# Quantised attention with its loop written out, two heads scored side by side, and its weights turned as pairs of bytes

## The reference, cut to what matters

```python
q = (x @ Wq + bq).reshape(1, B * N, H, hd)
kv = (cond @ Wkv + bkv).reshape(1, -1, 2, H, hd)
...
q = _fq_sym(q, axis=-1)        # rounded to -127..127 times a scale
k = _fq_sym(k, axis=-1)
v = _fq_sym(v, axis=2)
attn = jnp.einsum('bhqd,bhkd->bhqk', q, k)
attn = jax.nn.softmax(attn.astype(jnp.float32), axis=-1)
attn = _fq_unsigned(attn, axis=-1)   # each row: round(w / (max/255)), 0..255
out = jnp.einsum('bhqk,bhkd->bqhd', attn, v)
return out @ Wp + bp
```

## Time and profile before

| | us |
|---|---|
| median of 3 runs | 3037.68 (3037.57 to 3043.3) |
| profiled execution | 3038.51 |
| its span, first to last instruction | 3036.7 |
| VectorE busy over the span | 1932.5 (64%) |
| TensorE busy over the span | 2498.7 (82%) |
| ScalarE busy over the span | 1482.0 (49%) |
| GpSimd busy over the span | 409.3 (13%) |

### The profile page before, as it was taken

How to read it: one execution, slowest core, us unless ns; L and a number is a source line. 1 busy time by engine, 2 the same in 40 slices (tenths; PEclk the granted TensorE clock), 3 DMA queues, 4 the chain that set the end, 5 groups by cost and what they waited for, 6 DMA issues and landing times. The chain is left out here.

```text
span 3036.7 us, 50228 instructions
## 1 busy us (share of the span) xinstructions
PE 2498.7 (82%) x16570; PEld 1358.9 (45%) x16570; DVE 1932.5 (64%) x3686; ACT 1482.0 (49%) x2055; POOL 409.3 (13%) x454
## 2 busy tenths in 40 slices
PE   6874775999979999999664888787878865999998
PEld 3333554555547777777552222222222232444444
DVE  6995556667743333333456998888888845666665
ACT  5552332444433333333232776666666633666664
POOL 0001220111012222333133000000000001001100
PEclk9886776999979999999776555555555567999999
DMA  2000000000010000000000999999999940000001
GB/s 83 0 0 19 0 0 12 16 26 21 21 29 18 18 17 17 17 17 9 21 0 18 177 176 169 165 169 162 171 163 171 173 71 17 24 23 16 23 23 36
DMA packets 594876, 175.35 MB, mean 58 GB/s; under 512 B 548642, under 2 KB 594212, under 8 KB 594724
## 3 DMA queue, kind: packets, MB, share of 16 engines
q1 hardware_dynamic: 594724, 173.44, 29.6%
HBM read 37.07 MB, written 2.10 MB: 13 GB/s over the span
## 5 line engine op out<-in xcount | busy, mean ns | idle before, releaser
L1682 DVE TENSOR_SCALAR_CACHE_REDUCE ctxT<-psum,e_nsq 128x1024 f32<-128x1024 f32 x512 | 637.2, 1282 | 74.2 <-issue 54.1
L1651 PE MATMUL psum<-e_KT,e_Qs 48*128 48x512 bf16 x1024 | 519.9, 611 | 181.7 <-DVE ctxT L1682 151.0
L1703 ACT ACTIVATE xh<-ctxT,e_ebias 128x2048 uint16<-128x2048 f32 x128 | 256.2, 2002 | 134.0 <-DVE e_ebias L1686 134.0
L1703 ACT ACTIVATE xl<-ctxT,e_ebias 128x2048 uint16<-128x2048 f32 x128 | 256.2, 2002 | 119.2 <-DVE e_ebias L1686 119.2
L1651 PEld LDWEIGHTS psum<-e_KT,e_Qs 48*128 48x128 bf16 x1024 | 67.3, 104 | 415.8 <-issue 408.1
L103 PE MATMUL psum<-xh,d_WT 128*128 128x512 f16 x768 | 229.4, 381 | 2.6 <-DVE d_WT L1214 2.6
L1662 PEld LDWEIGHTS psum<-e_Vi,xnT 128*128 128x128 f16 x4096 | 129.5, 105 | 216.8 <-issue 216.8
L1233 DVE TENSOR_TENSOR d_ACC<-psum,d_ACC 128x512 f32<-128x512 f32 x128 | 82.5, 686 | 171.1 <-PE psum L1287 171.1
L103 PE MATMUL psum<-xh,f_WA 128*128 128x512 f16 x544 | 152.7, 383 | 13.9 <-DVEq L1896 11.8
L103 PE MATMUL psum<-xh,c_Wx 128*128 128x512 f16 x576 | 161.3, 383 | 0.8 <-DVE X L960 0.8
L1662 PE MATMUL psum<-e_Vi,xnT 128*128 128x16 f16 x4096 | 152.5, 175 | 8.1 <-DMA xnT<-xh 4.5
(11 more groups left out here) (312 smaller groups left out, 4965.9 us busy)
## 6 DMA issues: line engine op xcount, KB each, us to landing
d_Wn<-in_L_attn_w_qkv SPq DMA_DIRECT2D x16, 384.0 KB, 3.2
f_W<-in_L_ffn_w_routed SPq DMA_DIRECT2D x32, 176.0 KB, 2.5
ctx_rows<-in_ctx SPq DMA_DIRECT2D x1, 2048.0 KB, 8.6
X<-in_x SPq DMA_DIRECT2D x1, 2048.0 KB, 14.0
c_Wgu<-in_L_ffn_rg SPq DMA_DIRECT2D x16, 128.0 KB, 2.1
c_Wgu<-in_L_ffn_rw SPq DMA_DIRECT2D x16, 128.0 KB, 2.2
c_Wd<-in_L_ffn_rw SPq DMA_DIRECT2D x16, 128.0 KB, 2.2
d_Wn<-in_L_attn_w_gate SPq DMA_DIRECT2D x16, 128.0 KB, 3.0
```

The costliest lines, as they stand in the source:

```text
L1651: mm = pe.matmul(m.bank[b + q], Qs[rows, x.u // 2 % QSLOTS, :], KTt[rows, j // 2, (2 * hf + q) * BLK:(2 * hf + q + 1) * BLK], start=True, ...
L1682: dve.tensor_scalar(S32[:, sl, hf * HALF:(hf + 1) * HALF].rearrange("p (a b) -> p a b", a=2), m.psum[:, b:b + 2, :], nsq[:, ds(x.n(), 1)], ...
L1703: act.activation(e16[x.u % SLOTS], S32[:, x.u % 2, :], ACT.Exp, bias=ebias[:, x.u % 2:x.u % 2 + 1], scale=-1.0, accum_out=esum[:, ds(x.n() ...
```

## The change

- The loop is written out: 256 units on every engine, no hardware loop and no `wait_apart`; semaphores are waited for at constants. TensorE reads the queries straight from `e_QT`, and GpSimd's copies into `e_Qs` go.
- Two heads are scored at once: `score` is called once for two units and alternates the matmuls of the even head (rows 0 to 47) and the odd head (rows 64 to 111), each into banks of its own. The ring still has three pairs of banks, now counted in chunks (even half 0, odd half 0, even half 1, odd half 1). VectorE takes four chunks out per two units.
- The bias of the exponential moves from VectorE to GpSimd (L1598 of the changed kernel).
- ScalarE writes the integers as bytes; the DMA turns them as pairs, 8 blocks of 128 x 128 two-byte numbers a unit; GpSimd then casts 2048 bytes a row to bfloat16, in order (L1591), three units late (`LATE`). So that a pair of bytes belongs to two tiles of keys, ScalarE stores `e_KT` with the tokens of two tiles interleaved. TensorE reads the weights of a tile with a step of two numbers. `e_Vi` is bfloat16.
- Four slots instead of two for the scores (a new tensor `e_Smore`) and the biases; `LAG` is 7; the 2^24 is gone.

```diff
@@ -1385,7 +1385,7 @@
 
         QT = sb("QT", [P, NT * PR, P], BF16)
         KTt = sb("KT", [P, PR, TOK], BF16)
-        Vi = sb("Vi", [P, KT, H, HD], F16)
+        Vi = sb("Vi", [P, KT, H, HD], BF16)
         sq = sb("sq", [P, NT * H])
         nsq = sb("nsq", [P, NT * H])
         sv = sb("sv", [P, D])
@@ -1463,8 +1463,10 @@
                             b = 4 + 2 * (tt % 2)
                             act.activation(QT[:, ds(t * PR, PR), :].rearrange("p a b -> p (a b)"),
                                            m.bank[b].bitcast(BF16), ACT.Copy)
-                            act.activation(KTt[:, :, ds(t * P, P)], m.bank[b + 1].bitcast(BF16)
-                                           .rearrange("p (a b) -> p a b", a=PR), ACT.Copy).then_inc(stored, 1)
+                            act.activation(KTt[:, :, ds(i * 2 * TPB * P + tt // 2 * 2 * P, 2 * P)]
+                                           .rearrange("p a (q b) -> p a q b", b=2)[:, :, :, tt % 2],
+                                           m.bank[b + 1].bitcast(BF16).rearrange("p (a b) -> p a b", a=PR),
+                                           ACT.Copy).then_inc(stored, 1)
 
                 @block.vector
                 def _(dve):
@@ -1554,49 +1556,24 @@
 
 
         N = NT * H
-        BODY, SLOTS, LAG, QAHEAD, QSLOTS = 48, 4, 6, 3, 6
-        Qs = sb("Qs", [P, QSLOTS, P], BF16)
-        mn = sb("mn", [P, 2, 2])
-        ebias = sb("ebias", [P, 2])
+        SLOTS, LAG, LATE = 4, 7, 3
+        mn = sb("mn", [P, SLOTS, 2])
+        ebias = sb("ebias", [P, SLOTS])
         esum = sb("esum", [P, N])
         Osb = sb("Osb", [P, NT, D])
-
-
-        S32 = m.ctxT
-        PT = m.xnT[:, :, :].rearrange("p a b -> p (a b)").bitcast(F16).rearrange("p (s k q) -> p s k q", s=SLOTS, k=KT)
-        e16 = [x[:, :, :].rearrange("p a b -> p (a b)").bitcast(U16)[:, i * TOK:(i + 1) * TOK]
-               for x in (m.xh, m.xl) for i in range(2)]
-
-
...
-        def loop(eng, step, extra=0):
-
...
+        Smore = sb("Smore", [P, 2, TOK])
+
+
+        S32 = [m.ctxT[:, 0, :], m.ctxT[:, 1, :], Smore[:, 0, :], Smore[:, 1, :]]
+        PT = m.xnT[:, :, :].rearrange("p a b -> p (a b)").bitcast(BF16).rearrange("p (s k) -> p s k", s=SLOTS)
+        e8 = m.xh[:, :, :].rearrange("p a b -> p (a b)").bitcast(U8).rearrange("p (s k) -> p s k", s=SLOTS)
+        P8 = m.xl[:, :, :].rearrange("p a b -> p (a b)").bitcast(U16).rearrange("p (s c q) -> p s c q", s=SLOTS, c=KT // 2)
+
+
+        def loop(step, extra=0):
+
+            for n in range(N + extra):
+                step(n)
 
         def pair_banks(c):
 
@@ -1606,106 +1583,103 @@
             @block.gpsimd
             def _(pool):
 
...
+                def unpack(n):
+                    sl = n % SLOTS
+                    pool.wait_ge(laid[sl], 16 * (n // SLOTS + 1))
+                    if n >= SLOTS:
+                        pool.wait_ge(mixed, n - SLOTS + 1)
+                    pool.tensor_copy(PT[:, sl, :],
+                                     P8[:, sl, :, :].rearrange("p c q -> p (c q)").bitcast(U8)).then_inc(unpacked, 1)
+
+                def step(n):
+                    if n < N:
+                        sl = n % SLOTS
+                        pool.wait_ge(score_out, n // 2 * 4 + 3 + n % 2)
+                        pool.tensor_scalar(ebias[:, sl:sl + 1], mn[:, sl, 0:1], mn[:, sl, 1:2], LN255,
+                                           ALU.min, ALU.add).then_inc(biased, 1)
+                    if n >= LATE:
+                        unpack(n - LATE)
+                loop(step, LATE)
 
             @block.sync
             def _(sp):
-                def step(x):
-                    m.wait_apart(sp, exped, x.n() + 1)
-                    if x.at_least(SLOTS):
-                        m.wait_apart(sp, mixed, x.n() - (SLOTS - 1))
-                    sp.dma_start_transpose(PT[:, x.u % SLOTS, :, :], e16[x.u % SLOTS].bitcast(F16)).then_inc(laid[x.u % SLOTS], 16)
-                loop(sp, step)
+                def step(n):
+                    sl = n % SLOTS
+                    sp.wait_ge(exped, n + 1)
+                    if n >= SLOTS:
+                        sp.wait_ge(unpacked, n - SLOTS + 1)
+                    sp.dma_start_transpose(P8[:, sl, :, :], e8[:, sl, :].bitcast(U16)).then_inc(laid[sl], 16)
+                loop(step)
 
             @block.tensor
             def _(pe):
-                def score(x):
-                    j = x.j
-                    rows = slice(64 * (j % 2), 64 * (j % 2) + 48)
-                    if j % 2 == 0:
-                        m.wait_apart(pe, q_here, x.n(2) + 1)
+                def score(n):
+
                     for hf in range(2):
-                        if x.at_least(2):
-                            m.wait_apart(pe, score_out, x.n(1, 2) + hf - 2)
-                        elif 2 * x.u + hf >= 3:
-                            pe.wait_ge(score_out, 2 * x.u + hf - 2)
-                        b = pair_banks(2 * x.u + hf)
+                        c = 2 * n + 2 * hf
+                        if c >= 2:
+                            pe.wait_ge(score_out, c - 1)
                         for q in range(2):
-                            mm = pe.matmul(m.bank[b + q], Qs[rows, x.u // 2 % QSLOTS, :],
-                                           KTt[rows, j // 2, (2 * hf + q) * BLK:(2 * hf + q + 1) * BLK],
-                                           start=True, stop=True)
+                            col = (2 * hf + q) * BLK
+                            for odd in range(2):
+                                rows = slice(64 * odd, 64 * odd + 48)
+                                mm = pe.matmul(m.bank[pair_banks(c + odd) + q], QT[rows, n // 2, :],
+                                               KTt[rows, n % H // 2, col:col + BLK], start=True, stop=True)
                         mm.then_inc(scored, 1)
 
-                def mix(x):
-                    j = x.j
-                    m.wait_apart(pe, laid[x.u % SLOTS], x.n(SLOTS, 16) + 16)
-                    if j % 8 == 0 and x.at_least(16):
-                        m.wait_apart(pe, normed, x.n(8) - 1)
+                def mix(n):
+                    j = n % H
+                    pe.wait_ge(unpacked, n + 1)
+                    if j % 8 == 0 and n >= 16:
+                        pe.wait_ge(normed, n // 8 - 1)
                     for k in range(KT):
-                        mm = pe.matmul(m.bank[6 + j // 8][:, j % 8 * HD:(j % 8 + 1) * HD], PT[:, x.u % SLOTS, k, :],
+                        mm = pe.matmul(m.bank[6 + j // 8][:, j % 8 * HD:(j % 8 + 1) * HD], PT[:, n % SLOTS, k // 2 * 2 * P + k % 2:(k // 2 + 1) * 2 * P:2],
                                        Vi[:, k, j, :], start=(k == 0), stop=(k == KT - 1))
                     mm.then_inc(mixed, 1)
 
-                def step(x):
-                    if x.exists():
-                        score(x)
-                    if x.back(LAG).exists():
-                        mix(x.back(LAG))
-                loop(pe, step, LAG)
+                def step(n):
+                    if n % 2 == 0 and n < N:
+                        score(n)
+                    if n >= LAG:
+                        mix(n - LAG)
+                loop(step, LAG)
 
             @block.vector
             def _(dve):
-                def step(x):
-                    sl = x.u % 2
-                    if x.at_least(2):
-                        m.wait_apart(dve, exped, x.n() - 1)
+                def step(n):
+                    if n % 2:
+                        return
+                    if n >= SLOTS:
+                        dve.wait_ge(exped, n - SLOTS + 2)
                     for hf in range(2):
-                        b = pair_banks(2 * x.u + hf)
-                        m.wait_apart(dve, scored, x.n(1, 2) + hf + 1)
-                        dve.tensor_scalar(S32[:, sl, hf * HALF:(hf + 1) * HALF].rearrange("p (a b) -> p a b", a=2),
-                                          m.psum[:, b:b + 2, :], nsq[:, ds(x.n(), 1)], None, ALU.mult, ALU.min,
-                                          accum_out=mn[:, sl, hf:hf + 1]).then_inc(score_out, 1)
-                    m.wait_apart(dve, score_out, x.n(1, 2) + 2)
-                    dve.tensor_scalar(ebias[:, sl:sl + 1], mn[:, sl, 0:1], mn[:, sl, 1:2], LN255,
-                                      ALU.min, ALU.add).then_inc(biased, 1)
-                loop(dve, step)
+                        dve.wait_ge(scored, n + hf + 1)
+                        for odd in range(2):
+                            sl = (n + odd) % SLOTS
+                            b = pair_banks(2 * n + 2 * hf + odd)
+                            dve.tensor_scalar(S32[sl][:, hf * HALF:(hf + 1) * HALF].rearrange("p (a b) -> p a b", a=2),
+                                              m.psum[:, b:b + 2, :], nsq[:, n + odd:n + odd + 1], None, ALU.mult, ALU.min,
+                                              accum_out=mn[:, sl, hf:hf + 1]).then_inc(score_out, 1)
+                loop(step)
 
             @block.scalar
```

(86 more changed lines are left out.)

1 line of the change is left out of this document (removed).

## The result

The changed kernel takes 2875.77 us (median of 4; 2874.03 to 2879.97) against 3038.53 before: ratio 0.9463, 95% interval 0.9447 to 0.948. The forecast was 2910 in a range of 2850 to 3060, faster. The direction held, and so did the reading that VectorE's chain sets the pace; the gain was 163 us where 127 were worked out, and the stall at each turn-around with TensorE, on which the forecast rested, was nearly absent.

A forecast was written before the change was run, and what follows sets the result against it. VectorE's own chain was taken as the bound: 128 pairs x 5.22 = 668 against 795.9 gives -128, with -0.3 at the start and +1 at the tail -127, so 2910 us; range 2850 to 3060.

The forecast's parts named there:

- What bounds the kernel: VectorE's chain of two take-outs and a bias sets 3.10 us a unit; DMA near second, share 1.01 at 2.9.
- Two heads at once: Scoring: a group of four matmuls lasts 1.01 like two; a pair of units takes 5.22, a unit 2.61.
- the 1.40: TensorE-VectorE turn-around: 0.23 to the group's start plus 1.17 to VectorE's, against 1.21 for one take-out.
- Bias to GpSimd, loop written out: VectorE loses 256 biases of 213 ns, the wait before them and 0.23 gaps; two take-outs, 2.42 a unit, remain.
- The cast: GpSimd's cast of 2048 numbers takes 1.9 us; two units need 4.6 of 5.22, so it is covered.
- The mixes and the weights' step: TensorE's two mixes take 1.1 at 32 ns a load despite the stepped read; slack 0.6, so no cost.
- The rival's upper price: Stepped weight loads on TensorE at 107 ns each: 6.9 a pair of units, 3128 us; chance 4%.
- half-speed rival: Stepped weight loads on TensorE at 64 ns: next group 0.3 late, 5.5 a pair, 2950 us; chance 7%.
- The DMA: Transposes move 8 blocks instead of 16; landing between 4.3 and half of it, covered by about 5 us or more.
- The tail: End of block: last cast 1.9 and late bias 1.2 against about -2 of transpose: +1 on 9.3.
- The clock: TensorE's granted clock stays 0.50, as it will be busy about 3.2 of 5.22, less than today's 78%.
- a risen clock: Rival: TensorE's clock at 1.00, group about 0.6, no stall, VectorE at 2.42 a unit: 2861 us; chance 9%.

The follow-up runs named there:

- the step of eight: Changed kernel with TensorE's weights read eight numbers (16 bytes) apart instead of two, output differs: 2948.66 us.

## Why the prediction was right, and where its size was off

- *What bounds the kernel:* right. VectorE's chain set the pace before and does after. The DMA was the near second, but its capacity was misread: with sixteen bits it gave a unit in 2.64, not 2.93.
- *Two heads at once,* the term that was mis-sized: 2 x (1.40 + 1.21) = 5.22 a pair, measured 4.95. 128 x 0.27 is 35 us, and the forecast was 34 high. The stall of 0.19 at every turn-around did not come: 0.01 is left in the middle of a pair, and the 0.10 at its head is a second wait on one instruction. Both parts of the 1.40 were read from rows whose waits had a semaphore instruction beside them, which the change removes; with it back, 1.44 and 5.30 were measured. The diff named that instruction and I priced it only as part of "the loop's bookkeeping". The overlap of the row halves held (1.03 for four matmuls). But the pairing, for which that overlap was needed, bought nothing: one head at a time is as fast.
- *Bias to GpSimd, loop written out:* 0.68 a unit went, as said, but the kernel before gets 113 us by plain waits and the written-out loop alone. The move of the bias is worth 17 us in the changed kernel. With sixteen bits, pairs and moved bias together end at 2923, and the kernel before with plain waits at 2925.
- *The bytes:* worth 47 us in the changed kernel (2923 to 2876), because the chain had become shorter than the DMA's 2.64. The prediction's sum has no term for them.
- *The cast:* 1.89 forecast, 1.891 measured; the bias on GpSimd took 0.29, in its bounds. That an overloaded GpSimd makes the kernel slower than before is borne out (3095). The best case of 1.8 cycles a number in the Trainium skill ("GPSIMD Engine Reference", section 3.1) does not hold for this cast: 1.891 us less 0.19 is 1.0 cycles a number at the 1.2 GHz given there.
- *The mixes and the weights' step:* 32 loads in 0.93, no cost. The rival's upper price was misread. Its 107 ns a load come from a row where the granted clock was 1.00; at 0.50, the clock of this stage, the same eight loads take 1.57, 196 ns each (the kernel before):

```profile
297.59 1.57 PEld L731 LDWEIGHTS psum<-ident,b_S 128*128 128x128 f32 x8 [3.94 <-ACT b_S L610]
```

- The half-speed rival's 2950 and the 2949 of the step of eight agree by luck: the prediction had 5.22 and 0.3 a pair, the runs show 4.95 and about 0.6.
- *The DMA:* landing took 3.0, between its bounds. *The key store:* 1.31 instead of 1.0 each, and nothing waited for it. *The tail:* 10.0 from the last take-out, +0.6 where +1 was said. The first take-out came 1.2 earlier, not 0.3, but it lies between 1654.4 and 1657.4 over the runs, so that shows nothing.
- *The clock:* it stayed at 0.50, as forecast. The reason given, that TensorE would be busy for a smaller share, is not borne out: one head at a time kept TensorE on record as busy throughout, and the clock stayed there too. What keeps it low is open. A VectorE that never waits was named as the sign of a risen clock; it nearly came (busy 99.56 of 100 us), and in full with one head at a time, at 0.50. The 2861 priced for a risen clock was reached there without it.

## What to carry to other kernels

Before a turn-around is priced from a row, look at what stands between the two instructions on both engines: here the extra instructions beside the waits were worth 0.35 us a pair of units, and scoring two heads at once, a main idea of the change, was worth nothing. Look at the clock of a row, too, before its time is used at another. A wait belongs on an instruction that has none yet. And when the ring of banks lets the producer run two take-outs ahead, filling two at once gives up part of that lead, and here the pairing won nothing in exchange.
